# Value product of the clipped cross-attention layer: four heads per burst in four column groups, eight probability tiles

## What is computed

```python
# x + layer(layernorm(x), ctx_768): 8 batches, 256 queries, 512 keys, 16 heads of 8
q, k, v = x @ Wq + bq, ctx @ Wk + bk, ctx @ Wv + bv
logits = clip(q @ k^T * 8 ** -0.5, -1e4, 1e4)
attn = softmax(logits)
y = (attn @ v) @ Wo + bo
```

## Time and profile before

| | |
|---|---|
| median of 3 runs | 2568.94 us (2568.23 to 2571.85) |
| the profiled execution | 2570.0 us, span 2568.3 us, mean granted clock 0.868 |
| layer 1, from its first to its last value product | about 199 to 495 us of the span |
| PE, DVE, ACT, POOL busy over the whole span | 80%, 59%, 43%, 22% |

### The profile page before, as it was taken

The page is one execution under the profiler, slowest core; times in us unless marked ns, Lnnn a source line. Parts: engine busy times, 40 slices in busy tenths (PEclk is TensorE's granted clock), DMA queues, the critical chain, the costliest instruction groups (busy, mean ns, idle before and its releaser), DMA issues. The chain is left out here.

```text
span 2568.3 us, 37822 instructions
## 1 busy us (share of the span) xinstructions
PE 2047.7 (80%) x12547; PEld 1222.8 (48%) x12547; DVE 1516.6 (59%) x3578; ACT 1115.2 (43%) x2797; POOL 572.8 (22%) x803
## 2 busy tenths in 40 slices
PE   4759999879996886656999975656999996988872
PEld 2424444434443554444676653544666663444431
DVE  5748888644435553764767665753666663755534
ACT  3215555534323663323555533220666663555550
POOL 1033431100004420132111111002443432322100
PEclk9759999889995888888999997865999997788895
DMA  1043311286633211001000010101000002424210
GB/s 31 1 98 81 75 42 39 43 192 150 149 71 96 70 39 31 9 1 34 1 1 1 1 30 2 30 0 39 2 1 1 2 1 64 110 56 83 45 15 16
DMA packets 128698, 112.60 MB, mean 44 GB/s; under 512 B 62294, under 2 KB 101374, under 8 KB 126206
## 3 DMA queue, kind: packets, MB, share of 16 engines
q1 hardware_dynamic: 95230, 109.17, 18.3%
q10 hardware_dynamic: 33280, 1.05, 0.6%
HBM read 93.99 MB, written 15.20 MB: 43 GB/s over the span
## 5 line engine op out<-in xcount | busy, mean ns | idle before, releaser
L952 DVE TENSOR_REDUCE L_xattn_mx<-L_xattn_psS 128x1 f32<-128x512 f32 x512 | 327.7, 683 | 150.2 <-PE L_xattn_psS L1077 146.3
L1187 ACT ACTIVATE L_xattn_PT<-L_xattn_psT 128x512 f32<-128x512 f32 x512 | 285.0, 599 | 109.8 <-PE L_xattn_psT L1089 103.5
L598 ACT ACTIVATE L_attn_pr<-L_attn_psS,L_attn_negm 128x256 f32<-128x256 f32 (+1 forms) x512 | 222.4, 446 | 102.9 <-DVE L_attn_negm L398 67.1
L1077 PE MATMUL L_xattn_psS<-L_xattn_KR,L_xattn_QR 72*128 72x512 bf16 x512 | 221.8, 438 | 42.0 <-DVE L_xattn_mx L952 21.2
L396 DVE TENSOR_REDUCE L_attn_mx<-L_attn_psS 128x2 f32<-128x512 f32 x256 | 164.9, 685 | 115.8 <-PE L_attn_psS L507 115.7
L1089 PE MATMUL L_xattn_psT<-L_xattn_QR,L_xattn_KR 75*128 75x256 bf16 x1024 | 207.1, 289 | 3.4 <-ACT L_xattn_PT L1187 1.5
L1103 PE MATMUL L_xattn_psO<-L_xattn_PT,L_xattn_V 128*32 128x256 f32 x2048 | 195.6, 403 | 3.6 <-ACT L_xattn_PT L1187 1.1
L1956 DVE TENSOR_TENSOR L_ffn_act<-L_ffn_act,L_ffn_cwb 128x512 f32<-128x512 f32 x128 | 86.7, 690 | 129.5 <-ACT L_ffn_act L2086 105.9
L507 PE MATMUL L_attn_psS<-L_attn_qk 64*128 64x256 f32 x1024 | 146.6, 404 | 11.8 <-ACT L_attn_pr L598 11.8
L1089 PEld LDWEIGHTS L_xattn_psT<-L_xattn_QR,L_xattn_KR 75*128 75x128 bf16 x1024 | 104.2, 104 | 84.0 <-issue 22.2
L2021 PE MATMUL L_ffn_psU<-L_ffn_hT,L_ffn_wup 128*128 128x512 f32 x256 | 133.1, 610 | 13.8 <-ACT L_ffn_act L2086 13.8
(11 more groups left out here) (550 smaller groups left out, 4002.5 us busy)
## 6 DMA issues: line engine op xcount, KB each, us to landing
L_ffn_cwb<-L_ffn_weights_by_expert SPq DMA_DIRECT2D x64, 512.0 KB, 7.7
L_xattn_KR<-L_xattn_k_parts SPq DMA_DIRECT2D x96, 192.0 KB
L_xattn_QR<-L_xattn_q_parts SPq DMA_DIRECT2D x32, 288.0 KB
L_xattn_k_parts<-L_xattn_ks SPq DMA_DIRECT2D x48, 128.0 KB, 2.4
L_xattn_ctxT<-in_ctx SPq DMA_DIRECT2D x24, 192.0 KB, 2.3
L_attn_QR<-L_attn_q_parts SPq DMA_DIRECT2D x16, 288.0 KB
L_attn_KR<-L_attn_k_parts SPq DMA_DIRECT2D x48, 96.0 KB
L_xattn_q_parts<-L_xattn_qs SPq DMA_DIRECT2D x48, 64.0 KB, 2.0
```

What stands on the lines that cost most here:

```text
L598: ins = nc.scalar.activation(pr[n % 3][:, r, t, 0:width], psS[(2 * n + r) % 3][:, t, 0:width], ACT.Exp, bias=negm[:, n % 4, t, r:r + 1], s ...
L952: nc.vector.reduce_max(mx[:, b % 2, u, hd:hd + 1], psS[n % 2][:], AX.X).then_inc(s_used, 1)
L1077: ins = nc.tensor.matmul(psS[n % 2][:, i * keys:(i + 1) * keys], QR[b % NB][0:PAIR, hd, t * P:(t + 1) * P], KR[b % NB][0:PAIR, hd, :], sta ...
L1187: nc.scalar.activation(PT[n % NPT][:, 2 * u:2 * u + 2], psT[i % NPS][:], ACT.Exp).then_inc(exp_ready, 1)
```

## The change

```diff
-    WG = 2 if clamp else HG
-    NPS, NPT = 3, 5 if clamp else 8
+    WG = HG
+    NPS, NPT = 3, 8
```

## The result

The changed kernel takes 2594.74 us (median of four runs, 2593.86 to 2601.68), the kernel before 2568.59 beside it (four runs, 2559.66 to 2571.85). The ratio is 1.0113, with an interval of 1.0083 to 1.0144: 26 us slower. The forecast was 2570 within 2555 to 2585, so the time lies outside the range, and rival (b), the clock that falls twice or more in a batch, came true. Its two prices gave 2582 and 2603.

A forecast was written before the change was run, and what follows sets the result against it. PE (36.8 of 40.0 us busy) and DVE (34.0) both nearly full, odd steps bound by the burst, even ones by DVE; 2570.0 - 14.5 + 14 = 2569.5 profiled, median 2568.4, rounded to 2570, range 2555 to 2585.

The forecast's parts named there:

- rival (b): Clock falls twice in most batches or stays low longer, bursts after emptied steps paying 1.66 us: slower; chance 0.30.
- two prices: For 14 more clock falls: 2582 us at 2.0 us each, 2603 us at 3.5 us each.
- the number of falls: PE clock falls in layer 1: a little over one a batch, eight in the layer, seven more than now.
- The price: Cost of one PE clock fall in layer 1: 2.0 us taken, 3.5 as upper end; seven more cost 14 us.
- The sum at full clock: Gain in layer 1 if PE keeps its speed: 9.4 + 1.5 + 3.6 = 14.5 us.
- W3, W7, W11 and W15: Removed value-product bursts, numbered by step in the batch: gains 0, 0.90 (0.54 in batch 0), 0, 0.50; together 9.4 us.
- V and K: DVE's idle times in a batch before V (1.31 us) and behind a kept burst and K (1.32 us): unchanged.
- The end: Layer's end, paced by ACT's exponentials: four-head groups take 5.3 instead of 6.5 us; three removed bursts give 3.6 us.
- The start: Layer's start up to step 20: 1.5 us from the first burst plus idle times of 0.54 and 0.50 saved.
- The first burst: Layer's first burst, removed: 3.15 us at half clock, DVE idle 2.23 behind it; 1.5 us gain taken.
- W5: Kept burst at step 5, now four heads: may still meet the low clock at the start, at most 1.2 us more.
- rival (a): The clock holds through the emptied stretches, so the whole 14.5 us come: 2554.4 us; chance 0.28.

The follow-up runs named there:

- middle filled: The change, with throw-away repeats of the second half's turned scores in three of four steps, from the ninth head to step 113: 2555.38 us, ratio 0.9963.
- eight tiles: The kernel before with only the eight probability tiles, bursts still of two heads: 2565.56 us, ratio 0.9996.
- waste: The change with the removed two-head bursts run again, their results overwritten by the four-head bursts: 2570.24 us, ratio 1.0023.
- two heads without clipping: The kernel before with the clipping of the probabilities left out: 2548.07 us, ratio 0.9934.
- the halves: The change with each four-head burst split into two half bursts two steps apart; copy, turn and normalise two steps later: 2557.40 us, ratio 0.9971.
- the halves with filling: The change with its burst in two halves, plus throw-away repeats of turned scores in every second step: 2544.75 us, ratio 0.9929.

## Why the prediction was wrong

**The term that failed: the number of falls.** The forecast took "a little over one in a batch, eight in the layer". There were 22, over three in a batch. The reason given was that "after a fall PE is full for some us and covers the next stretch". The fullness is there (3.40 of 3.40 at 288.1), but it ends with the clock's rise: what was late is caught up, and the next stretch at DVE's pace is as empty as before. From 295.0 PE is at 1.74 of 3.30 again, and V's matmuls at 298.87 are already at half clock. The forecast had called all the emptied stretches emptier than the one that fell before, and then counted only one of them.

**The price was right.** The change and the kernel with its middle filled differ by 390.7 - 350.2 = 40.5 us in the layer and by 21 falls: 1.9 us each, against 2.0 taken. (This is a subtraction, with the cost of the filling in it.) With 22 falls instead of eight the forecast's own sum is 2570.0 - 14.5 + 21 x 2.0 = 2597.5 in the profiled execution (2601.68 measured) and 1.1 less in the median, 2596.4 (2594.74 measured). It comes out 4.2 us low in the profiled execution, about as much as the gain at full clock, next, was taken too high (4.3). Rival (b) had the mechanism and 14 more falls; its chance of 0.30 was too low next to 0.40 for a forecast that rested on the same emptied stretches.

**The sum at full clock.** 14.5 us were expected. With the middle filled the layer is 10.2 us shorter (360.4 - 350.2), and the measured 2555.38 lies 9.4 us below the kernel before. Point by point, in the kernel with the middle filled:
- W3, W7, W11 and W15: a batch takes 38.78 us, right within 0.2 us of 38.6. From the maxima of step 20 to the last ones it is 9.25 us shorter (before 240.31 to 467.28, with the middle filled 242.66 to 460.38), where 9.4 - 0.54 - 0.50 = 8.4 were forecast.
- V and K: DVE idles 1.31 and 1.34, as forecast.
- The end: bursts 5.35 and 5.23 us apart (473.72, 479.07, 484.30) against 5.3, right there. One of its bursts met a fall (466.23, 3.60 us), and from the last maxima to the layer's end it is 1.5 us shorter, not 3.6.
- **The start: 2.5 us expected, 0.5 lost.** Layer 1's first load is issued at 138.8 us before, at 140.1 in the change and at 140.7 with the middle filled, so its times are counted from there. The maxima of step 20 come after 101.5, 102.0 and 102.0 us; the forecast had them 1.5 + 0.54 + 0.50 = 2.5 earlier than before. With the 2.1 missing at the end and 0.9 gained too much between, this makes up the 4.3 us between 14.5 and 10.2.
- **The first burst: 1.5 expected, left open.** Before, the clock rose at 201.6, 62.8 us into the layer; in the change at 206.2, with the middle filled at 210.3. W5 then pays. The maxima of steps 3 and 6, with W5 between; in order the kernel before, the change, and the middle filled:

```profile
198.50 1.29 DVE L952 TENSOR_REDUCE L_xattn_mx<-L_xattn_psS 128x1 f32<-128x512 f32 x2
206.84 1.29 DVE L952 TENSOR_REDUCE L_xattn_mx<-L_xattn_psS 128x1 f32<-128x512 f32 x2 [0.54 <-PE L_xattn_psS L1077]
...
199.86 1.29 DVE L952 TENSOR_REDUCE L_xattn_mx<-L_xattn_psS 128x1 f32<-128x512 f32 x2
204.22 2.88 PE L1103 MATMUL L_xattn_psO<-L_xattn_PT,L_xattn_V 128*32 128x256 f32 x32
207.46 1.29 DVE L952 TENSOR_REDUCE L_xattn_mx<-L_xattn_psS 128x1 f32<-128x512 f32 x2 [1.66 <-PE L_xattn_psS L1077]
...
201.35 1.29 DVE L952 TENSOR_REDUCE L_xattn_mx<-L_xattn_psS 128x1 f32<-128x512 f32 x2
205.71 3.64 PE L1104 MATMUL L_xattn_psO<-L_xattn_PT,L_xattn_V 128*32 128x256 f32 x32
209.93 1.36 DVE L952 TENSOR_REDUCE L_xattn_mx<-L_xattn_psS 128x1 f32<-128x512 f32 x2 [2.63 <-PE L_xattn_psS L1077]
```

From step 3 to step 6 that is 8.34, 7.60 and 8.58 us: 0.7 gained in the change, 0.2 lost with the middle filled. By step 8 (211.06, 211.07 and 213.60) the gain is 1.35 and 0.31. Yet the last two kernels do the same up to step 8, so their difference is one between two executions and not between programs, and one execution of each can't size this term. That the missing burst delays the rise is argued, with this for it: the rise came 62.7 to 64.6 us into the layer in the four profiled executions that have a burst at step 3 (before, eight tiles, waste, two heads without clipping) and 65.9 to 72.9 us in the ten others, five of which also have filling there. No run has W3 back alone.

**At the end of the changed kernel** the 3.6 us did not come either: from the last maxima (498.03) to the layer's end it took 33.0 us, against 32.0 before, and the clock fell there too. Three of its last bursts:

```profile
511.49 2.85 PE L1103 MATMUL L_xattn_psO<-L_xattn_PT,L_xattn_V 128*32 128x256 f32 x32
517.75 1.93 PE L1103 MATMUL L_xattn_psO<-L_xattn_PT,L_xattn_V 128*32 128x256 f32 x32
522.98 3.06 PE L1103 MATMUL L_xattn_psO<-L_xattn_PT,L_xattn_V 128*32 128x256 f32 x32 [1.89 <-DVE L_xattn_PT L960]
```

**The argument for rival (a)** was that the layer had passed such a stretch six times of seven. It had passed one with PE 2.10 of 3.40 busy, and the trace has one more like it:

```profile
368.90:372.30 3.40, 2.10 (x18) 1.72 (x16) 2.22 (x4) 1.46 (x3) 0.00 (x0) 1.00 0.00 0
```

In the other batches the place was fuller (2.30 at 327.9, 2.32 at 290.4), so the six passes were fewer than they seemed, and none says much of stretches with 1.3. In the changed kernel 2.02 in 240.3 to 243.7 is followed by a fall. The loads that I foresaw for the emptied stretches were read well (1.3, seen 1.29; 1.6, seen 1.64 at 250.6); what they would do was not.

The Trainium skill has a section that I had not weighed. TensorE: Matmul & The Clock Gate, section A second HAM failure mode: psum-queue depth-cycling, tells of a kernel in which "the PE micro-idles between MM groups frequently enough that HAM oscillates" (HAM is the page's name for what gates TensorE's clock, MM is a matmul). The trace agrees: 22 falls in the layer, while PE's longest wait between scores in the batch shown is 1.15 us, before V 1.76, and in the whole layer from 205 us on 1.91. The rule on single gaps, which the forecast had cited from the same page, would have given no fall.

**What stays open.** Where between 0.22 and 0.66 us of filling a step the falls go: doses between were not run. Why two falls of the halves lasted 17.1 and 13.7 us with PE busy nearly throughout. What the removal of the first burst is worth. And whether real work could take the place of the wasted turned scores.

## What to carry to other kernels

Before work is taken off PE, ask who paces it. If another engine does (here DVE, 34.0 of 40.0 us), the freed time becomes idle time of PE, and the clock may take back more than the edit gives: count the stretches that the edit empties, and charge each one a fall (here 1.9 us) rather than one a batch. A saving in one lump is better spread: two halves had 9 falls where one burst had 22, and with the emptiest steps filled by repeated matmuls the same saving became a gain of 1.0%. Leave low-clock stretches such as a layer's start out of the filling, and fill enough or not at all.

## What the runs showed of the hardware

- Wasted matmuls can pay: 63 us of unread bursts made the change 24.5 us faster, and repeated scores in the middle of the layer 39.4 us faster (2594.74 to 2555.38).
- The effect is not in proportion to the work: 22 falls without filling, 21 with one repetition a step up to step 113, 2 with three.
- In the change a fall lasted 3.4 or 6.8 us, once 10.2 (22 falls for 109.2 us, 5.0 us each). So falls recur, and none of the page's slices from the fourth to the eighth is below 7 tenths: a mean of 0.82 is a series of short falls. It isn't so everywhere: in the halves two of nine lasted 17.1 and 13.7 us, with PE busy for 16.23 and 13.50 of them.
- Two profiled executions can differ in layers that no edit touches: the halves with filling showed 2519.61 us once, in a layer 10 of 325.0 us instead of the 347.1 of the kernel before (the other profiled executions have 341 to 352), and its median is 2544.75. The time of the edited layer between its boundaries was the steadier measure.
